# Contexts of the attention in seven groups per head instead of ten, in a four-stage kernel on one Trainium2 core

## The reference, cut to what matters

```python
scores = jnp.einsum('bhqd,bhkd->bhqk', q, k)
scores = jnp.where(causal, scores, neg)
attn = jax.nn.softmax(scores, axis=-1)
ctx = jnp.einsum('bhqk,bhkd->bhqd', attn, v)
```

## Time and profile before

| | us |
|---|---|
| median of 3 runs | 1946.15 (1944.91 to 1947.98) |
| the profiled execution | 1946.09 |
| its span on the core | 1944.3 |
| first attention's heads, about | 510 to 942 |
| second attention's heads, about | 1271 to 1704 |
| one pair of heads in the middle | 55.4 |

### The profile page before, as it was taken

One profiled execution on the slowest core, in us unless ns is written; L12 is line 12 of the kernel. 1 busy time (PEld: TensorE's weight loads), 2 busy tenths in 40 slices (PEclk: granted clock), 3 DMA queues, 4 the chain that ended last, 5 costly groups with the idle time before them and its releaser, 6 DMA issues.

```text
span 1944.3 us, 28236 instructions
## 1 busy us (share of the span) xinstructions
PE 1526.5 (79%) x8103; PEld 660.5 (34%) x8104; DVE 1270.9 (65%) x2848; ACT 884.0 (45%) x1663; POOL 411.3 (21%) x267
## 2 busy tenths in 40 slices
PE   4817766634999999999623933599999999949999
PEld 2302222221233333333322822133333333236665
DVE  2379999666888888886250115688888888343444
ACT  2353323101477777777401311077777777821121
POOL 5009989511011110000224042001011110100000
PEclk9968889966799999999756976599999999969999
DMA  2012212104111111110151121311111110000001
GB/s 73 1 35 75 77 65 76 66 1 123 38 45 44 50 41 46 37 50 14 30 156 48 54 45 45 109 34 51 47 41 37 50 50 25 14 17 10 23 17 30
DMA packets 59073, 91.77 MB, mean 47 GB/s; under 512 B 13001, under 2 KB 39057, under 8 KB 58993
## 3 DMA queue, kind: packets, MB, share of 16 engines
q1 hardware_dynamic: 56962, 86.79, 15.2%
q0 software_dynamic: 2048, 4.20, 0.9%
HBM read 74.63 MB, written 16.32 MB: 47 GB/s over the span
## 4 chain that ended last, share of the span: by engine, by line
PE 67%; DVE 20%; ACT 4%; POOL 4%; issue 3%; DMA 2%; SPq 1%; DVEq 1%; POOLq 0%; ACTq 0%
PE psum_a L876 17%; PE psum_a L858 14%; PE psum_b L846 11%; DVE arena L516 5%; DVE arena L490 4%; PE psum_a L1515 3%; PE psum_b L1515 3%; PE psum_b L326 2%; PE psum_a L326 2%; PE psum_b L1524 2%; ACT psum_a L432 2%; PE psum_a L1524 2%; POOL expert_inputs L1265 2%; DVE extra L1047 2%; POOL arena L1271 2%
## 5 line engine op out<-in xcount | busy, mean ns | idle before, releaser
L986 ACT ACTIVATE arena<-psum_a 128x512 f32<-128x512 f32 (+3 forms) x1280 | 594.8, 537 | 194.0 <-PE psum_a L858 103.2
L1047 DVE TENSOR_REDUCE extra<-psum_b 128x1 f32<-128x512 f32 x768 | 486.6, 683 | 71.8 <-PE psum_b L846 70.0
L846 PE MATMUL psum_b<-arena 72*128 72x512 bf16 (+3 forms) x1280 | 422.9, 368 | 53.2 <-DMA arena<-k_parts 51.5
L858 PE MATMUL psum_a<-arena 75*128 75x512 bf16 (+3 forms) x1280 | 415.5, 353 | 3.7 <-ACT arena L986 3.7
L876 PE MATMUL psum_a<-arena,extra 128*32 128x512 f32 x2560 | 342.7, 607 | 1.8 <-ACT arena L986 1.4
L1044 DVE CUSTOM_DVE_ANT_0 extra<-psum_b,mask_q 128x512 bf16<-128x512 f32 (+3 forms) x512 | 224.5, 486 | 78.1 <-PE psum_b L846 65.3
L858 PEld LDWEIGHTS psum_a<-arena 75*128 75x128 bf16 x1280 | 118.5, 98 | 350.8 <-ACT arena L986 287.2
L295 POOL TENSOR_TENSOR arena<-arena,extra 128x1024 f32<-128x1024 f32 x48 | 170.9, 3573 | 130.3 <-DVE arena L516 118.2
L846 PEld LDWEIGHTS psum_b<-arena 72*128 72x128 bf16 x1280 | 118.8, 100 | 172.3 <-DMA arena<-k_parts 51.8
L792 POOL TENSOR_TENSOR arena<-arena 128x512 f32<-128x512 f32 x64 | 81.6, 1275 | 415.0 <-ACT arena L977 281.0
L977 ACT ACTIVATE arena<-psum_a 128x512 f32<-128x512 f32 x128 | 76.4, 597 | 93.9 <-PE psum_a L876 93.9
(11 more groups left out here) (263 smaller groups left out, 1666.3 us busy)
## 6 DMA issues: line engine op xcount, KB each, us to landing
arena<-q_parts SPq DMA_DIRECT2D x192, 96.0 KB
arena<-k_parts SPq DMA_DIRECT2D x192, 96.0 KB
extra<-c_rows SPq DMA_DIRECT2D x32, 512.0 KB, 3.6
arena<-in_L_ffn_fc_w_dram SPq DMA_DIRECT2D x32, 256.0 KB, 6.0
k_parts<-arena SPq DMA_DIRECT2D x10, 512.0 KB, 5.7
q_parts<-arena SPq DMA_DIRECT2D x6, 512.0 KB, 4.9
arena<-in_L_ffn_w_dram SPq DMA_DIRECT2D x24, 128.0 KB, 2.1
expert_inputs<-zeros SPq DMA_DIRECT2D x4, 512.0 KB, 6.3
```

The costliest lines, as they stand in the source:

```text
L846: m = e.matmul(ps[:, at:at + width], s.mq[0:ROWS, b, i * P:(i + 1) * P], s.mk[0:ROWS, b, c * CW:c * CW + width], start=True, stop=True)
L858: m = e.matmul(score_bank(p)[:, at:at + width], s.ek[0:ROWS + 3, b, j * P:(j + 1) * P], s.eq[0:ROWS + 3, b, (c + 1) * CW - width:(c + 1) * ...
L986: m = e.activation(probabilities(s, b, kind, quad, k, width), score_bank(p)[:, at:at + width], ACT.Exp)
L1047: m = e.tensor_reduce(s.mpart[:, i, c:c + 1], ps[:, at:at + length], AX.X, ALU.max)
```

## The change

The list `SETS` is written out with seven entries per head. Three pairs of quads go together:

```diff
-        SETS = []
-        for c in range(NC):
-            SETS += [(c, [("diagonal", c)])] + [(c, [("full", c * (c - 1) // 2 + f)]) for f in range(c)]
+        SETS = [(0, [("diagonal", 0)]), (1, [("diagonal", 1), ("full", 0)]), (2, [("diagonal", 2)]), (2, [("full", 1), ("full", 2)]),
+                (3, [("diagonal", 3)]), (3, [("full", 3)]), (3, [("full", 4), ("full", 5)])]
```

## The result

| | before | after |
|---|---|---|
| median, us | 1947.07 (1944.91 to 1948.85, 4 runs) | 1967.26 (1963.65 to 1973.07, 4 runs) |
| ratio | | 1.0107 (95% interval 1.008 to 1.0134) |
| profiled execution, us | 1946.09 | 1973.07 |
| span, us | 1944.3 | 1971.2 |
| a pair of middle heads, us | 55.36 | 56.48 |

The kernel is slower by 20 us, 1.07%. The same kernel was run once more beside the experiments: 1968.67 (1963.82 to 1971.36, 5 runs), ratio 1.0106 (1.0092 to 1.012). Forecast were 1970.7, in 1955 to 1984.

A forecast was written before the change was run, and what follows sets the result against it. PE was taken as the bound; merges save 17.8 us, but waits for DVE and ACT and losses in the last pair outweigh this, +12.3 us a layer, +24.6 in all: 1946.09 to 1970.7 us, range 1955 to 1984.

The forecast's parts named there:

- The bound: Whole kernel: PE waits for nobody, so what leaves PE's path shortens it and what makes PE wait lengthens it.
- The wait at step 20: Row of the maxima: PE arrives 1.09 us earlier and waits for DVE's chain, 0.69 us without turns, 1.09 with.
- Steps 6 to 9 and 32 to 35: PE waits for exponentials: 0.23 us (0.32 with turns) in steps 6 to 9, 0.12 in steps 32 to 35.
- The saving of a merge: Second quad in a set needs neither entry nor exit: 0.185 us saved a merge, bounds 0 to 0.24; 96 merges, 17.8 us.
- The last pair: Each layer's last two heads, where ring pieces run out: +1.09 us for the head with turns, +1.53 for the last.
- The sum: Per head +0.48 us without turns, +0.97 with; last pair 2.62; 12.3 a layer, +24.6 us in all.
- The saving arrives and nobody is met: Rival: the waits are shorter than read and the merges' 17.8 us arrive, 1928.3 us; chance 0.05.
- The second quad doesn't flow: Rival: each quad in a merged set pays as if alone, no saving, +42.4 us, 1988.5; chance 0.05 for more than half.
- The waits are met in part: Rival: ACT and DVE give back the waits of steps 6 to 9 and 32 to 35, 1960 us; chance 0.05 below 1955.
- The clock falls: Rival: waits over 1 us in 14 heads halve PE's clock for 8 us each, 56 us, 2027; chance 0.02.

The follow-up runs named there:

- the filled kernel: Changed kernel plus unread score products ahead of the wait for the last split, four in a pair's first head, one in its second: 1964.35 us, ratio 1.0094.
- the fastest kernel: Kernel before with seven sets: diagonal quad 1 merged with full 0, diagonal 2 with full 1 in step 16, full 4 with 5: 1941.60 us, ratio 0.9981.
- its version with the later row: Kernel before, ten sets unchanged, with the row of the maxima one ring piece later: 1945.55 us, ratio 0.9993.

## Why the prediction was right, step by step

**The bound.** PE sets the pace and waits for next to nobody before; PE starts to wait after. Right: the distances between the rows of the maxima carry the whole effect within a layer, 7.11 and 7.13 us in the repeat.

**The wait at step 20.** Forecast 0.69 and 1.09, measured 0.69 and 1.13. Four runs bear on it: the merge alone loses 25 us; the row moved behind the context, with all three merges kept, takes the whole loss back; the turn taken out of DVE's chain takes back 0.48 us a pair. And where a context stays in step 16 with as many merges, the row of the maxima waits for nobody. The mechanism is shown: the context of step 16 filled the time that DVE's chain needs.

**Steps 6 to 9 and 32 to 35.** Forecast 0.23 or 0.32 and 0.12; measured 0.235 or 0.32 and 0.155 to 0.165, each merge by itself.

**The saving of a merge was mis-sized.** This is the step that failed: 0.185 us was taken, with 0.24 as the upper bound, and 0.23 came. I took the distance of two passes within a set (0.453) for every further pass, though a set's second pass was the only one to read. In the run of eight the passes come in turn 0.45 and 0.43 apart:

```profile
747.67 0.64 PE L875 MATMUL psum_a<-arena,extra 128*32 128x512 f32 x4
748.12 1.04 PE L875 MATMUL psum_a<-arena,extra 128*32 128x512 f32 x8
748.55 1.04 PE L875 MATMUL psum_a<-arena,extra 128*32 128x512 f32 x8
```

Of a layer's 48 merges 43 have their saving ahead of its last row of the maxima: three in each of 14 heads and that of step 9 in the head after them. In both layers that is 86 x 0.045 = 3.9 us. The forecast had 2 x (12.3 - 2.87) = 18.9 us there; 15.0 are left, and the repeat has 14.24. The rest goes with the 0.15 us a pair by which the three merges together cost less than apart, and which stays open. The pair of middle heads was to be 56.8 to 57 and is 56.48.

**The last pair.** From the last row of the maxima to the end of the heads (the first product of the sum behind the last context) 2.87 us a layer were forecast (0.91 + 0.43 + 1.53). Before, the stretch is 34.20 us in both layers. In the filled kernel's second layer, where no drop falls into it, it is 36.97: 2.77. In the changed kernel it is 40.06 and 38.27, in the repeat 38.30 and 41.23, with one or two drops each. So this term was right and a cost not in it came on top.

**The sum.** Without the drops the steps come to 14.24 + 2 x 2.77 = 19.8 us, five less than the 24.6 forecast. Of the profiled execution's 26.9 us, 16.15 lie between the rows of the maxima (one drop of 1.67 among them), 9.93 in the last stretches and 0.8 elsewhere. Its heads come near the forecast by luck: 6.1 us of drops, which were not in the sum, make up for the five that it had too much. That the medians moved by 20.2 us, close to 19.8, is no proof of the smaller sum either: the heads in the repeat's profile are 25.4 us longer than before, drops included, and the rest of that execution is 2.8 us shorter than in the profile before.

**The rivals.** *The saving arrives and nobody is met:* ruled out by the waits; where the one of step 20 is taken away with all merges kept (1945.29 us), only 0.23 us a pair come through, since steps 6 to 9 and 32 to 35 and the scores ahead of step 20 keep their waits. *The second quad doesn't flow:* ruled out, 1.86 us a set against the 2.1 from which it would have decided. *The waits are met in part:* each merge by itself meets its waits in full; together they cost 0.15 us a pair less, far from the 0.35 a head of this rival. *The clock falls:* right in kind and far off in size. It falls for 3.4 us at a time, once for 6.8, and not for 8, in three or four places and not in 14, and costs some 6 us and not 56.

## What to carry to other kernels

Work that an engine does between a producer's start and the consumer's wait is cover, and moving it behind the wait costs the whole of it, however cheap the move looks; count from the producer's last wait to the consumer's start what stands between, on both engines. When groups are merged, merge those that leave something between the two, or move the consumer behind the merged group: here that is a difference of 20 to 27 us. An engine that is busy all the time can still be faster, between its breaks, than the engines beside it. Taking the breaks away then buys less than they cost, unless work of those engines goes as well. And look at a loop's last rounds by themselves: where work of the rounds ahead is missing, the same move had another price (here 2.1 us a layer in the last stretch even for the fastest kernel).

## What the runs showed of the hardware

- The granted clock of TensorE drops to half for 3.4 us (6.8 in two places; those at the end of the heads run on into what follows) inside the heads, during or within some three microseconds behind waits of 0.26 to 1.9 us, and not at each such wait: the kernel before waits 1.3 us at 909 at full clock, and its version with the later row has a drop at just that place (its window 908 to 915, stretches, in the fence below). The place changes from one execution to the next. Only two drops in all these profiles lie outside a layer's last two heads, both right behind a wait of 0.8 us for the row of the maxima; four profiles, that of the kernel before among them, have none in their heads. One costs 1.7 us if a set of two falls into it.
- Fp32 passes of 512 columns in 32-column quarters come 0.45, 0.43 and 0.43 us apart in a run of two quads, and a second quad costs 0.86 us where a single one costs 1.09.
- From the end of the heads to the end of the program the profiles have 236.9 to 241.6 us, whatever the kernel, and each kernel that was run twelve times ranges over 11 us and more (1941.22 to 1955.70 for seven sets with the row one entry later). A single execution can't tell 0.2%. Where that comes from was not looked into.

```profile
908.00:915.00 7.00, 5.69 (x29) 1.22 (x27) 1.78 (x7) 3.69 (x10) 0.00 (x0) 0.76 0.02 4
```
